# A graph-attention kernel on one core: the operands of two long comparisons move to PSUM

## The reference, cut to what matters

```python
h  = relu(layernorm(x)) @ W_node.T                 # per node, 4 heads x 32
att = leaky_relu(sum(concat(h[src], h[dst], edge_attr @ W_edge.T) * a), slope 0.2)
m   = max(segment_max(att, dst), 0)
ex  = exp(att - m[dst])
den = segment_sum(ex, dst) + (n_edges - degree) * exp(-m)
out = x + segment_sum(ex / den[dst] * h[src], dst)
```

## Time and profile before

| what | us |
|---|---|
| median of 3 runs | 2149.22 (2147.46 to 2149.89) |
| the profiled execution, its own time | 2149.45 |
| its span in the profile | 2147.6 |
| first gather of `h_table` starts | 70.17 |
| last gather of `h_table` starts | 2098.39 |
| end after it | 49.2 |

### The profile page before, as it was taken

One profiled execution on the slowest core, in us unless ns is written; L12 is line 12 of the kernel. 1 busy time (PEld: TensorE's weight loads), 2 busy tenths in 40 slices (PEclk: granted clock), 3 DMA queues, 4 the chain that ended last, 5 costly groups with the idle time before them and its releaser, 6 DMA issues.

```text
span 2147.6 us, 39173 instructions
## 1 busy us (share of the span) xinstructions
PE 1319.3 (61%) x9599; PEld 1202.2 (56%) x9600; DVE 1561.3 (73%) x4654; ACT 817.3 (38%) x2329; POOL 1584.2 (74%) x1674
## 2 busy tenths in 40 slices
PE   6466666666656666666666655665665665666665
PEld 6456655565655555555555555555555555655554
DVE  8768878887667667667677676676676776776777
ACT  7434444433333333333333343243343333333333
POOL 7677777777777777777777777777777777777770
PEclk9757777776666766666666666666666666566666
DMA  9663333333333333333333333333333333333320
GB/s 293 165 232 111 93 111 98 104 110 90 90 106 90 90 108 89 88 108 90 88 108 90 89 107 90 90 108 88 95 103 88 101 97 87 106 93 87 108 71 28
DMA packets 119885, 224.74 MB, mean 105 GB/s; under 512 B 40373, under 2 KB 80181, under 8 KB 113093
## 3 DMA queue, kind: packets, MB, share of 16 engines
q0 software_dynamic: 53440, 113.99, 22.3%
q1 hardware_dynamic: 65565, 110.07, 15.4%
q10 hardware_dynamic: 848, 0.35, 0.1%
HBM read 180.28 MB, written 43.98 MB: 104 GB/s over the span
## 4 chain that ended last, share of the span: by engine, by line
POOL 73%; issue 24%; DVE 1%; DMA 1%; POOLq 1%; DVEq 0%; PE 0%; ACT 0%; SPq 0%; ACTq 0%
POOL gath L488 71%; POOL gath L461 2%; DMA gath<-in_x_rows,idx 0%; DVE vals L831 0%; POOLq L282 0%; POOLq L286 0%; DMA h_table<-onehot 0%; DMA gath<-h_table,idx 0%; DVEq L80 0%; DVE rows_mem L718 0%; DVE bank_rn L714 0%; PE bank_w L1127 0%; DVE x_all L890 0%; DMA idx<-in_src 0%; ACT onehot L979 0%
## 5 line engine op out<-in xcount | busy, mean ns | idle before, releaser
L488 POOL DMA_INDIRECT gath<-h_table,idx x1621 | 1535.5, 947 | 501.9 <-issue 493.7
L1198 PE MATMUL bank_t<-ident_b,onehot_bits 128*128 128x128 bf16 x1672 | 188.7, 282 | 387.2 <-DVE onehot_bits L725 369.2
L1231 PE MATMUL bank_p<-vals,onehot 128*128 128x137 f32 x1664 | 408.0, 438 | 0.4
L1231 PEld LDWEIGHTS bank_p<-vals,onehot 128*128 128x128 f32 x1664 | 380.8, 330 | 5.5
L1198 PEld LDWEIGHTS bank_t<-ident_b,onehot_bits 128*128 128x128 bf16 x1672 | 150.5, 130 | 413.9 <-DVE onehot_bits L725 389.7
L1074 ACT COPY onehot_bits<-bank_t 128x1024 bf16<-128x1024 bf16 x209 | 211.5, 1012 | 350.9 <-PE bank_t L1198 325.7
L725 DVE SCALAR_TENSOR_TENSOR onehot_bits<-bank_w,tables,zz 128x1024 bf16 (+1 forms) x209 | 268.3, 1284 | 20.6 <-issue 1.9
L1231 PE MATMUL bank_w<-vals,onehot 128*128 128x137 f32 x1664 | 280.1, 333 | 0.6 <-DVE vals L831 0.6
L1231 PEld LDWEIGHTS bank_w<-vals,onehot 128*128 128x128 f32 x1664 | 260.4, 236 | 14.7 <-DVE vals L831 14.5
L1208 PE MATMUL bank_s<-s_live,onehot_bits 128*128 128x24 bf16 x1672 | 75.0, 177 | 249.4 <-ACT onehot_bits L1074 249.4
L1173 PEld LDWEIGHTS bank_z<-w_edge_bd,ef 128*128 128x128 f32 x1664 | 217.7, 214 | 17.2 <-DMA ef<-in_edges 17.2
(11 more groups left out here) (167 smaller groups left out, 1991.6 us busy)
## 6 DMA issues: line engine op xcount, KB each, us to landing
ef<-in_edges SPq DMA_DIRECT2D x52, 1024.0 KB
out_x<-x_all SPq DMA_DIRECT2D x210, 128.0 KB
gath<-h_table,idx POOLq DMA_INDIRECT x1621
x_all<-in_x SPq DMA_DIRECT2D x14, 448.0 KB, 12.5
out_x<-x_all SPq DMA_DIRECT2D x14, 448.0 KB, 11.3
h_table<-gath SPq DMA_DIRECT2D x12, 462.0 KB
resets<-ef SPq DMA_DIRECT2D x8, 416.0 KB
flag_rows<-resets SPq DMA_DIRECT2D x52, 64.0 KB, 2.0
```

The source lines that it names most:

```text
L488: e.indirect_dma_start(gath[:, q * GPS + g, t * ROW:(t + 1) * ROW], None, table, bass.IndirectOffsetOnAxis(idx[:, q, g * TILES + t:g * TIL ...
L1198: ins = e.transpose(bank_t[:, :].bitcast(BF16)[:, t * P:(t + 1) * P], onehot_b[buf][:, t, :], ident_b[:, :])
L1231: ins = e.matmul(half_p[q], onehot[q][:, t, :], vals[q][:, t, :], start=(t == 0), stop=(t == TILES - 1))
```

## The change

ScalarE, after its last eviction, copies one operand of L612 to PSUM in three pieces (1023 columns into `bank_rn`, 512 into `bank_p`, 511 into `bank_s`), and one operand of L622 in four (512, 512, 512 and 128 columns into `bank_w[0]`, `bank_w[1]`, `bank_t` and `bank_z`). A new semaphore `n_turned` counts the seven copies. VectorE waits for the first three, makes the first comparison in three instructions, and the second in four, waiting before each for its copy and after each for its own end (`chain`). The waits on `n_flags` count two higher.

```diff
+        turned_rows = ((bank_rn, 0, 0, GROUP - 1), (bank_p, 1, 0, 512), (bank_s, 1, 512, 511))
+        turned_next = [(bank, slice(64 * k, min(64 * k + 64, GROUPS)))
+                       for k, bank in enumerate((bank_w[0], bank_w[1], bank_t, bank_z))]
@@ SyncE
-                wait(e, n_flags, 3 + k)
+                wait(e, n_flags, 5 + k)
@@ VectorE
             wait(e, n_mm, 3 * ALL_CHUNKS)
-            e.wait_ge(d_rows, 16)
+            wait(e, n_turned, 3)
             inner = first_all[:, :, 1:GROUP]
-            e.tensor_tensor(inner, dst_rows[:, :, 0:GROUP - 1], dst_rows[:, :, 1:GROUP],
-                            ALU.not_equal).then_inc(n_flags, 1)
-            wait(e, n_flags, 1)
+            for bank, g, at, n in turned_rows:
+                e.tensor_tensor(inner[:, g, at:at + n], bank[0:GROUPS // 2, 0:n],
+                                dst_rows[:, g, at + 1:at + 1 + n], ALU.not_equal
+                                ).then_inc(n_flags, 1)
+            wait(e, n_flags, 3)
...
-            chain(e.tensor_tensor(is_last[:, :, :], dst_f[:, :, :], dst_next, ALU.not_equal))
+            for k, (bank, gs) in enumerate(turned_next):
+                wait(e, n_turned, 4 + k)
+                n = gs.stop - gs.start
+                chain(e.tensor_tensor(
+                    is_last[:, gs, :], dst_f[:, gs, :],
+                    bank[:, 0:n * TILES].rearrange("p (g t) -> p g t", t=TILES), ALU.not_equal))
@@ ScalarE
             rows_out(ALL_CHUNKS - 1)
-            wait(e, n_flags, 2)
+            wait(e, n_arow, rows_before(ALL_CHUNKS))
+            e.wait_ge(d_rows, 16)
+            for bank, g, at, n in turned_rows:
+                e.copy(bank[0:GROUPS // 2, 0:n], dst_rows[:, g, at:at + n]).then_inc(n_turned, 1)
+            wait(e, n_relu, 2 * ALL_CHUNKS)
+            e.wait_ge(d_dst, 32)
+            for bank, gs in turned_next:
+                n = gs.stop - gs.start
+                e.copy(bank[:, 0:n * TILES].rearrange("p (g t) -> p g t", t=TILES), dst_next[:, gs, :]
+                       ).then_inc(n_turned, 1)
+            wait(e, n_flags, 4)
             e.copy(last_all[:, :, 0:GROUP - 1], first_all[:, :, 1:GROUP]).then_inc(n_last, 1)
```

More of the change, by code:

```diff
@@ L251, in build @@
             "scan_b released stepped")
-        n_sqrt, n_relu, n_arow, n_last, z_ready = own_sems(
-            "ACT", "", "n_sqrt n_relu n_arow n_last z_ready")
+        n_sqrt, n_relu, n_arow, n_turned, n_last, z_ready = own_sems(
+            "ACT", "", "n_sqrt n_relu n_arow n_turned n_last z_ready")
         n_t, n_mm, r_full, e_mm, z_back_done = own_sems(
```

## The result

The changed kernel takes 2146.17 us (median of 20 runs, 2142.8 to 2147.88), the kernel before 2148.53 us (20 runs, 2147.46 to 2150.68). The ratio is 0.9988, 95% interval 0.9983 to 0.9994: 2.4 us gained, with 1.3 to 3.7 us in the interval. That is under the 0.2% named in the prediction, and clear of zero only because of the 20 runs. 2148.0 us was forecast, 2145.0 to 2151.0 as the range.

A forecast was written before the change was run, and what follows sets the result against it. GpSimd's stream of 1621 gathers was taken as the bound. Holds removed, -2.47 us, and phase, +1.2 us, gave -1.3 us: 2148.15 from the profiled 2149.45, 2147.9 from the median 2149.22; forecast 2148.0 us, range 2145.0 to 2151.0.

The forecast's parts named there:

- What bounds the kernel: GpSimd's unbroken stream: its start, 1621 gathers at a 1.25 us beat, and the tail set the time.
- The two holds go: Gathers at L612 and L622, 2.13 and 2.22 us long, fall to 0.94 us each: 2.47 us off the stream.
- rival B: Nothing gained at the comparisons: SBUF operand not the cause, or new form holds too; 2149.2 or 2150.4 us, chance 0.14.
- ScalarE's copies: After ScalarE's last eviction, the three copies for L612 take 2.24 us; the other four hide behind VectorE's work.
- VectorE's delay: Waiting for copies and running pieces makes everything behind L622 on VectorE some 4.1 us later, the flags 3.5 us.
- The cover: Slack before the 89th gather needs `released`: 16.8 us before, about 11 us after, so VectorE's lateness costs 0.
- Phase: Shifted short VectorE operations behind L622 meet gather starts: 1.9 us lost instead of 0.69, so 1.2 us given back.
- the walk: Gather beat stepped against VectorE's timeline moved 2.5 to 6 us, counting operations over gather starts: 1.4 to 2.6 us lost.
- Rival D: More gained: short operations miss the gathers and the loop's long beats shrink; 2145.5 to 2147 us, chance 0.2.
- The tail: What follows the last gather's start, 49.2 us; longer than that was named a sign against the prediction.
- wrong altogether: Sign that the prediction fails: the stream starts later than 70.17 us, or the tail is longer than 49.2 us.
- The first gather's start: Start of GpSimd's stream, forecast to stay at 70.17 us; a later start was a sign against the prediction.

The follow-up runs named there:

- e5: Kernel before, loop bounds asserted, with the first comparison made four more times, both operands in SBUF: 2156.27 us, ratio 1.0015 to the kernel before.
- e3: Changed kernel, loop bounds asserted, with copies, waits and pieces kept but all seven comparisons reading both operands from SBUF: 2152.2 us, ratio 0.9995 to the kernel before.
- a0: Changed kernel with its loop bounds asserted at load, otherwise the same: 2150.32 us, ratio 0.9992 to the kernel before.
- e7: Changed kernel, loop bounds asserted, first comparison (one operand in PSUM) made eight more times, on the slower chip: 3241.08 us, ratio 1.0156 to the kernel before.
- b0: Kernel before with only its loop bounds asserted at load: 2153.55 us, ratio 1.0004 to the kernel before.
- e6b: Repeat of the changed kernel, loop bounds asserted, first comparison made four more times, on the slower chip: 3244.42 us, ratio 1.0125 to the kernel before.
- e1: Changed kernel, loop bounds asserted, second comparison put back whole in SBUF, on the slower chip: 3217.27 us, ratio 1.0065 to the kernel before.

## Why the prediction was right, point by point

- **What bounds the kernel**: right. The stream of gathers and its beat set the time; a loss of 4.27 us inside the stream (e5) showed as 2.7 us in the medians, and the 9.3 us by which VectorE was later did not show.
- **The two holds go (-2.47 us)**: right in cause. e3 beside a0, e5, and the seven gathers of e7 show that the operand in SBUF holds and the one in PSUM doesn't, and rival B with its no gain falls. The sentence of the Trainium skill, "SBUF — State Buffer", section "Who interferes with whom", that a `tensor_tensor` stalled no DMA in a probe does not hold for these gathers, and the measurement decides: each of e5's five first comparisons stalled one. The Trainium skill's other sentence there, that two SBUF inputs contend with a GpSimd instruction that reads SBUF, fits them; the gather has its row numbers in SBUF. Of the prediction's two rows for PSUM operands one is evidence, the gather of 174.63. L725 began 0.03 us after that of 178.38, and an operation that begins after the gather doesn't hold it whatever it reads (see the phase below). What the prediction did not see is the share of the pieces. They were costed at nothing but fixed parts, while a cut comparison also lets a gather through between pieces (e3).
- **ScalarE's copies**: estimated at 2.24 us, measured 2.05 us (82.12 to 84.17).
- **VectorE's delay**: measured against ScalarE's last eviction, since this execution was 0.8 us early as a whole. The second comparison ended 3.77 us after it before (86.70 - 82.93) and 7.74 us after (89.83 - 82.09): 4.0 us later, forecast 4.1. L707 of before (L717) started at 119.66, or 120.5 with those 0.8 us, forecast 120.6.
- **The cover**: forecast at about 11 us, measured 11.7 us (the 89th gather at 180.43, `released` after the scan that ends at 168.76). No wait of GpSimd over 0.3 us appears, as forecast.
- **Phase (1.2 us given back)**: this is the term that was mis-sized. Forecast losses behind the comparisons were 1.9 us, L615's included, against 0.69 before; measured 0.94 us, in both executions of the changed kernel. So 0.25 us was given back, not 1.2. The step that failed is the rule by which the walk counted: "each gather whose first 0.13 us fall into such an operation". The rows show a narrower one. Every gather of 0.99 us or more in the six executions of the table, between 79 and 116 us, has an operation over its start that had already begun and had over 0.13 us left. Where one begins within those 0.13 us, the gather takes 0.94 to 0.95 us. In the changed kernel that is L633 (0.04 us after the start of the gather of 89.81), in e3 it is L622 (0.11 us after that of 87.22), and in the kernel before the scan L626 (0.12 us after that of 87.82):

```profile
87.82 0.94 POOL L488 DMA_INDIRECT gath<-h_table,idx  x1 [0.30 <-issue]
```

```profile
87.94 0.59 DVE L626 TENSOR_TENSOR_SCAN vals<-vals,onehot_bits 128x208 f32<-128x208 f32 x1
```

The walk, done again over the same rows (VectorE's timeline moved by 2.5 to 6 us in steps of 0.1), gives 1.5 to 2.4 us by the prediction's rule and 0.6 to 1.5 us, 1.0 in the mean, with only the operations that already run. An estimate by either rule still counts too much, as some kinds of operation don't hold: in the changed kernel L664 has 0.39 us left when the gather of 105.40 starts, and that gather takes 0.94 us. With 0.25 the sum is -2.47 + 0.25 = -2.2 us, which is what the stretch shows.
- **Rival D (a kind phase)**, at 0.2 and with 2145.5 to 2147 us, is where the time of 2146.17 us landed, in part by luck. Of the 1.8 us between forecast and result 0.7 us are the base: the kernel before has a median of 2148.53 us in 20 runs and had 2149.22 in the three that the forecast started from. The gain of 2.4 us lies just under D's 2.5. D's first half came true: the later holds were missed. Its second half did not happen: the loop lost 4.31 us after 115 us, not less than the 3.11 before.
- **The tail**: a tail over 49.2 us was named a sign of "wrong altogether", and it was 49.5 us in both executions of the changed kernel. The sign was set without room for scatter: b0, the kernel before again, has 50.2.
- **The first gather's start**: forecast unchanged, 68.89 instead of 70.17 in this profile, and 71.39 and 70.01 in b0 and a0. That is scatter ahead of the stream, where the gather waits for the table's DMA. Why it scatters was not sought.

## What to carry to other kernels

Where GpSimd's indirect DMAs are the bound, read its timeline beside VectorE's and look for gathers that end a fixed time after a VectorE operation does: each lengthens the stream, however idle the engines seem otherwise. An operand in PSUM ends that. The mere cut of a long operation into pieces seems to end part of it and needs no copy; e3's rows speak for it, but no run had the cut alone. To forecast what a shift of the timelines will do, count only operations that already run when a gather starts. Before moving work to another engine for it, read how much cover the moved engine has in front of the next thing that the bound waits for; on the slower chip here that cover was gone.

## What the runs showed of the hardware that was not expected

- **The beat differs between executions.** The median gather of b0, e3 and e5 is 947 ns and the shortest 942 to 943; of before and a0 they are 944 and 940. b0 and before are the same kernel but for the asserted bounds. Three nanoseconds on 1621 gathers are 4.9 us, twice the effect of the change. This goes with the column "after 115" in the table (6.2 to 6.9 us against 2.9 to 3.1).
- **One chip took 3202 us for a program that took 2150 us on others**, and the four kernels tried beside it took 3202 to 3248 us there. GpSimd started its stream 28 to 31 us later and waited for VectorE some 1000 us in the ring (e6b: 632.2, 330.4 and 55.6 us). Between 30 and 70 us e1's DMAs moved 147 GB/s there, where a0's moved 247 on its chip. The cause was not sought.
- **VectorE is held, too.** The same operation behind the comparison takes 0.33 us or 0.54 us, by where it lies to a gather. In VectorE's timeline of the changed kernel

```profile
92.76 0.33 DVE L646 TENSOR_SCALAR vals<-vals,step_cols 128x208 f32<-128x208 f32 x1
...
94.34 0.54 DVE L646 TENSOR_SCALAR vals<-vals,step_cols 128x208 f32<-128x208 f32 x1
...
96.13 0.33 DVE L646 TENSOR_SCALAR vals<-vals,step_cols 128x208 f32<-128x208 f32 x1
```

the long one runs from 94.34 to 94.88, over the end of the gather of 93.84 to 94.78. The two others lie in the first part of a gather and in the pause between two, up to the first 0.12 us of the next. L659 and L660 show it as well, 0.36 and 0.57 us where before the same two took 0.58 and 0.36. That a gather's last part is what holds VectorE is a reading of these few rows, and no run was made for it.
- **A scan of 208 numbers with both inputs in SBUF** (L636, 90.88 to 91.47) seems to hold a gather as well: that of 91.06 ends at 92.23, 0.76 us after it; in a0 the gather of 91.67 ends at 92.83, 0.75 us after the same scan.
